# A two-layer transformer stack with routed experts on one core: expert weights fetched and given back in smaller parts

## The reference

```python
# H, F, E, K = 512, 800, 8, 2
logits = xt @ gate_w.T
probs = softmax(logits)
top_vals, top_idx = top_k(probs, K)            # 2 of 8 experts for each token
top_vals = top_vals / sum(top_vals)
h1 = einsum('th,efh->tef', xt, w1)             # up projections, 512 -> 800
h3 = einsum('th,efh->tef', xt, w3)
act = silu(h1) * h3
expert_out = einsum('tef,ehf->teh', act, w2)   # down projection, 800 -> 512
y = einsum('te,teh->th', w_full, expert_out)   # weighted sum over each token's two experts
# and in the stack: x = x + 0.5 * y
```

## Time and profile before

| | |
|---|---|
| runs | 1313.04, 1319.79, 1327.81 us; median 1319.79 us |
| profiled execution, its own time | 1325.27 us |
| its span, from the first to the last instruction | 1323.3 us |
| mean granted TensorE clock | 0.947 of full speed |
| TensorE busy | 1189.0 us (90%) |
| moe stages, first to last expert matmul | 212.30 to 514.6 us and 978.07 to 1299.7 us |
| moved by the SP queue (q1) | 148.50 MB |

### The profile page before, as it was taken

One profiled execution on the slowest core, in us unless ns is written; L12 is line 12 of the kernel. 1 busy time (PEld: TensorE's weight loads), 2 busy tenths in 40 slices (PEclk: granted clock), 3 DMA queues, 4 the chain that ended last, 5 costly groups with the idle time before them and its releaser, 6 DMA issues.

```text
span 1323.3 us, 26791 instructions
## 1 busy us (share of the span) xinstructions
PE 1189.0 (90%) x9913; PEld 509.8 (39%) x9913; DVE 871.6 (66%) x2479; ACT 357.2 (27%) x739; POOL 141.4 (11%) x191
## 2 busy tenths in 40 slices
PE   7799787999999995896899999998989899999982
PEld 4477463433333331342334433433634223333320
DVE  5731466877777762876788888851459576777753
ACT  5433520000000001331166666665200000000010
POOL 2200011111111100441000000000110010111000
PEclk9799779999999998998999999999989989999996
DMA  9000324158714254239604332004841644514555
GB/s 367 26 1 1 147 88 164 49 171 301 253 59 148 97 169 183 110 107 166 109 12 84 53 53 30 2 2 165 340 180 35 245 143 176 201 57 184 191 183 211
DMA packets 49017, 174.22 MB, mean 132 GB/s; under 512 B 8558, under 2 KB 15300, under 8 KB 44920
## 3 DMA queue, kind: packets, MB, share of 16 engines
q1 hardware_dynamic: 39679, 148.50, 34.9%
q0 software_dynamic: 5760, 18.88, 4.3%
q10 hardware_dynamic: 3448, 5.14, 1.1%
HBM read 785.47 MB, written 22.03 MB: 610 GB/s over the span
## 4 chain that ended last, share of the span: by engine, by line
PE 74%; DVE 10%; DMA 9%; issue 3%; ACT 3%; SPq 1%; ACTq 0%; POOL 0%; POOLq 0%; DVEq 0%
PE PS L1006 27%; PE PS L1024 13%; PE PS L1483 5%; PE PS L1446 5%; PE PS L1470 4%; DMA arena<-split_scratch 3%; PE PS L747 3%; DMA HH<-in_w 3%; PE PS L730 3%; PE PS L1510 2%; PE PS L1398 2%; PE PS L515 2%; DVE PS L1604 2%; PE PS L1035 1%; PE PS L529 1%
## 5 line engine op out<-in xcount | busy, mean ns | idle before, releaser
L1006 PE MATMUL PS<-arena 128*32 128x400 f32 x3456 | 395.8, 501 | 10.1 <-DMA HH<-in_w 6.1
L1006 PE MATMUL PS<-HH,arena 128*32 128x400 f32 x1152 | 395.2, 501 | 0.0
L1006 PEld LDWEIGHTS PS<-arena 128*32 128x32 f32 x3456 | 143.5, 110 | 256.4 <-issue 250.1
L1604 DVE CUSTOM_DVE_ANT_0 PS<-PS,U 128x128 f32<-128x128 f32 (+7 forms) x256 | 188.4, 782 | 43.9 <-PE PS L1446 42.3
L1190 DVE STREAM_TRANSPOSE arena<-arena 32x192 f32<-32x192 f32 x576 | 211.4, 367 | 7.2
L1024 PE MATMUL PS<-arena 128*32 128x512 f32 x1512 | 197.3, 604 | 11.6 <-DMA arena<-in_w2a 9.6
L1551 ACT ACTIVATE arena<-PS 128x512 f32<-128x512 f32 (+3 forms) x384 | 165.0, 497 | 74.5 <-PE PS L1473 48.9
L1168 DVE STREAM_TRANSPOSE arena<-arena 32x128 f32<-32x128 f32 x544 | 164.7, 303 | 17.1 <-DMA arena<-h_scratch,RT 9.2
L1062 ACT ACTIVATE arena<-PS 128x400 f32<-128x400 f32 x72 | 36.3, 504 | 442.3 <-PE PS L1006 442.3
L1174 DVE TENSOR_TENSOR arena<-arena,PS 128x400 f32<-128x400 f32 x72 | 40.9, 571 | 142.5 <-ACT arena L1062 142.4
L1006 PEld LDWEIGHTS PS<-HH,arena 128*32 128x32 f32 x1152 | 125.0, 110 | 0.0
(11 more groups left out here) (247 smaller groups left out, 1248.3 us busy)
## 6 DMA issues: line engine op xcount, KB each, us to landing
arena<-in_w SPq DMA_DIRECT2D x228, 1600.0 KB
arena<-in_w2a SPq DMA_DIRECT2D x114, 1536.0 KB
HH<-in_w SPq DMA_DIRECT2D x76, 1600.0 KB
HH<-in_w2a SPq DMA_DIRECT2D x38, 768.0 KB
arena<-in_w2a SPq DMA_DIRECT2D x38, 768.0 KB
arena<-split_scratch SPq DMA_DIRECT2D x60, 128.0 KB, 5.7
split_scratch<-arena SPq DMA_DIRECT2D x8, 768.0 KB, 5.9
arena<-in_w2b SPq DMA_DIRECT2D x72, 64.0 KB
```

Source lines behind the costliest of these rows:

```text
L1006: mm = eng.matmul(PS[SR * j:SR * j + SR, 2 * hf + m, 0:FH], XBT[:, u, c, SR * j:SR * j + SR], W13[j][:, c // 2, m, c % 2, hf * FH:(hf + 1) ...
L1604: eng.tensor_tensor_reduce(scores, scores, MASKW[:, T - wide:T], 1.0, HOLE, ALU.add, ALU.max, MP[:, g % 2, h, i:i + 1]).then_inc(S("s_md"), 1)
```

## The change

The up weights of a stream are now loaded in four parts, one for each c, each with its own semaphore, and TensorE raises m_wf after each of c = 0, 1, 2 (the last part is still given back with m_h at the end of up). The down weights are loaded in two halves, each with its own semaphore; TensorE raises the new m_w2f after the first three of its six parts, and waits for the second half only ahead of part 3. The bytes stay the same. An up load of one stream was 2 x 1600 KB with rows of 6400 B and is 4 x 800 KB with rows of 3200 B; the down weights of streams 0 to 2 were 1536 KB with rows of 12288 B and are 2 x 768 KB with rows of 6144 B (stream 3's were so before). `guess_in` uses the same smaller parts.

```diff
--- before.py
+++ after.py
@@ -821,13 +821,13 @@
 
 
         xg_in = [sem("xg_in0"), sem("xg_in1")]
-        w13_in = [sem("w13_in0"), sem("w13_in1")]
-        w2_in = sem("w2_in")
+        w13_in = [sem(f"w13_in{c}") for c in range(C)]
+        w2_in = [sem("w2_in0"), sem("w2_in1")]
         y_out = [sem("y_out0"), sem("y_out1")]
         yl_in = [sem(f"yl_in{i}") for i in range(NT)]
         LOADS = NSTEP + 1
         N13 = 16 * NSTR
-        N2 = 16 * (NSTR + 1)
+        N2 = 16 * NSTR
         N2B = 16 * NSTR
         w2b_in = [sem("w2b_in0"), sem("w2b_in1")]
         assert NSTEP % 2 == 0
@@ -846,21 +846,22 @@
             r = (j + p % 2) % NSTR
             return slice(SR * r, SR * r + SR)
 
-        def up_in(eng, j, a, e, cond=None):
-
-            eng.dma_start(W13[j][:, a].rearrange("p m c f -> p m (c f)"),
-                          A["w13"][e, :, :, 2 * a:2 * a + 2].rearrange("e p m c f -> p (e m) (c f)"),
-                          cond=cond).then_inc(w13_in[a], 16)
-
-        def down_in(eng, j, e, cond=None):
-
-            at = 0
-            for part in W2A[j]:
-                n = part.shape[1]
-                eng.dma_start(part.rearrange("p c d -> p (c d)"),
-                              A["w2a"][e, :, at:at + n].rearrange("e p c d -> p (e c d)"),
-                              cond=cond).then_inc(w2_in, 16)
-                at += n
+        def up_in(eng, j, c, e, cond=None):
+
+            eng.dma_start(W13[j][:, c // 2, :, c % 2], A["w13"][e, :, :, c].rearrange("e p m f -> p (e m) f"),
+                          cond=cond).then_inc(w13_in[c], 16)
+
+        def half_of(j, half):
+
+            if len(W2A[j]) == 2:
+                return W2A[j][half]
+            return W2A[j][0][:, half * FC // 2:(half + 1) * FC // 2]
+
+        def down_in(eng, j, half, e, cond=None):
+
+            eng.dma_start(half_of(j, half).rearrange("p c d -> p (c d)"),
+                          A["w2a"][e, :, half * FC // 2:(half + 1) * FC // 2].rearrange("e p c d -> p (e c d)"),
+                          cond=cond).then_inc(w2_in[half], 16)
 
         def tail_in(eng, p, j, e):
 
@@ -872,9 +873,10 @@
 
         def guess_in(eng, f, j):
 
-            for a in range(2):
-                up_in(eng, j, a, guess(j))
-            down_in(eng, j, guess(j))
+            for c in range(C):
+                up_in(eng, j, c, guess(j))
+            for half in range(2):
+                down_in(eng, j, half, guess(j))
 
         def sp_moe(eng, k, f):
             h, last = HS[k][0], 2 if f == 0 else 3
@@ -895,23 +897,26 @@
                         q = j * NSTEP + p
                         x = eng.value_load(EBX[q:q + 1, 0:1], min_val=0, max_val=2 * NE - 1)
                         now.append((bass.ds(x % NE, 1), x >= NE))
-                    for a in range(2):
+                    for c in range(C):
                         if p == 0:
-                            eng.wait_ge(w13_in[a], N13 * (LOADS * f + 1))
-                        elif a == 0:
-                            eng.wait_ge(S("m_wf"), NSTEP * f + p)
+                            eng.wait_ge(w13_in[c], N13 * (LOADS * f + 1))
                         else:
-                            eng.wait_ge(S("m_h"), 2 * (NSTEP * f + p))
+                            done = NSTEP * f + p - 1
+                            if c < C - 1:
+                                eng.wait_ge(S("m_wf"), (C - 1) * done + c + 1)
+                            else:
+                                eng.wait_ge(S("m_h"), 2 * done + 2)
                         for j in range(NSTR):
-                            up_in(eng, j, a, *now[j])
+                            up_in(eng, j, c, *now[j])
                 if p >= 1:
                     q = p - 1
-                    if q == 0:
-                        eng.wait_ge(w2_in, N2 * (LOADS * f + 1))
-                    else:
-                        eng.wait_ge(S("m_w2"), NSTEP * f + q)
-                    for j in range(NSTR):
-                        down_in(eng, j, *late[j])
+                    for half in range(2):
+                        if q == 0:
+                            eng.wait_ge(w2_in[half], N2 * (LOADS * f + 1))
+                        else:
+                            eng.wait_ge(S(("m_w2f", "m_w2")[half]), NSTEP * f + q)
+                        for j in range(NSTR):
+                            down_in(eng, j, half, *late[j])
                     if q >= 2:
                         eng.wait_ge(S("m_y"), NSTEP * f + y_done(q - 2))
                     for j in range(NSTR):
@@ -998,8 +1003,7 @@
                 if G > 0:
                     eng.wait_ge(S("m_act"), 2 * G)
                 for c in range(C):
-                    if c % 2 == 0:
-                        eng.wait_ge(w13_in[c // 2], N13 * (LOADS * f + p + 2))
+                    eng.wait_ge(w13_in[c], N13 * (LOADS * f + p + 2))
                     for hf in range(2):
                         for m in range(2):
                             for j in range(NSTR):
@@ -1009,20 +1013,24 @@
                                                 start=(c == 0), stop=(c == C - 1), skip_group_check=True)
                         if c == C - 1:
                             mm.then_inc(S("m_h"), 1)
-                    if c == 1:
+                    if c < C - 1:
                         mm.then_inc(S("m_wf"), 1)
 
             def down(p):
                 G, u = NSTEP * f + p, p % 2
-                eng.wait_ge(w2_in, N2 * (LOADS * f + p + 2))
                 eng.wait_ge(S("m_at"), G + 1)
                 if G >= 2:
                     eng.wait_ge(S("m_yc"), G - 1)
                 for c in range(FC):
+                    half = 2 * c // FC
+                    if c == half * FC // 2:
+                        eng.wait_ge(w2_in[half], N2 * (LOADS * f + p + 2))
                     for j in range(NSTR):
-                        part = W2A[j][c // W2A[j][0].shape[1]]
                         mm = eng.matmul(PS[SR * j:SR * j + SR, 4 + u, :], ACT_T[:, u, c, SR * j:SR * j + SR],
-                                        part[:, c % part.shape[1], :], start=(c == 0), stop=False, skip_group_check=True)
+                                        half_of(j, half)[:, c % (FC // 2), :], start=(c == 0), stop=False,
+                                        skip_group_check=True)
+                    if c == FC // 2 - 1:
+                        mm.then_inc(S("m_w2f"), 1)
                 mm.then_inc(S("m_w2"), 1)
                 if paired(p) and p % 2 == 0:
                     return
```

## The result

| | before | changed |
|---|---|---|
| median of the runs, us | 1324.3 (1313.04 to 1327.81, 6 runs) | 1306.75 (1304.39 to 1313.84, 6 runs) |
| ratio, with its 95% interval | | 0.9884 [0.9855, 0.9913] |
| profiled execution, own time, us | 1325.27 | 1311.64 |
| its mean granted TensorE clock | 0.947 | 0.952 |
| first moe stage, first to last expert matmul | 302.3 | 301.2 |

The kernel is 1.2% faster; 1305 was forecast. The profiled executions differ by 13.6 us, and the second moe stage alone by 13.5. The first gives 1.0, and about 1 is given back outside the two.

A forecast was written before the change was run, and what follows sets the result against it. TensorE was taken to bound the kernel, with gains only where it waits. Terms of 2.5 + 6.5 + 6.4 + 0.5 = 15.9 us took the median 1319.79 to 1303.9, stated as 1305; range 1298 to 1317.

The forecast's parts named there:

- A: In up(4) of the second moe stage, where two streams change expert, up weights by quarters win 2.5 us.
- B: In down(4) of the second stage, where two streams change, down halves end the wait and low clock: 6.5 us.
- C: In down(17), the second stage's last, where one stream changes, down halves remove idle time and low clock: 6.4 us.
- first stage: In the first moe stage the 0.5 us wait for up weights goes; the 2.0 us set by VectorE stay.
- a gap of 2.04 us left the clock full: At A, two gaps of some 2.4 us were taken to leave TensorE at full clock.
- The 1 us that I kept back for it: Allowance for the clock at A, taken off the summed gain to give 1305 us.
- margin of 1.9 us: At B, time by which the second down half was to land before TensorE needs it.
- More parts to issue: On SP, eleven more loads cost 4.3 us a step, hidden in 6.7 us of waiting, leaving 2.4; cost 0.
- 1, the low clock behind the gaps: Rival: clock stays low in the cut-up waits at A and C; won 11.3 us, 1308.5; chance 0.14.
- 2, SP as the bound: Rival: more issues make SP set the step; slower, 1365 or 1338 us; chance 0.05.
- 3, a fixed time for every DMA: Rival: parts pay some 2 us each in series at A, B and C; gain 2 us, 1318; chance 0.06.
- 4, less without the profiler: Rival: waits are shorter without the profiler, or cause the runs' spread; half the gain, 8 us, 1312; chance 0.13.

The follow-up runs named there:

- experiment 3: The changed kernel run once more with no edit; 1307.22 us, ratio 0.9898 to the kernel before.
- experiment 6: Changed kernel with SP reading each step's four expert numbers twice; the second of two runs measured 1355.17 us, ratio 1.0255.
- experiment 1: Kernel before with only the down weights by halves, up weights still in two halves; 1314.73 us, ratio 0.9899.
- experiment 4: Changed kernel with both down halves asked for only when all six parts of the down before are done; 1315.83 us, ratio 0.9941.
- first profile of 7: Changed kernel with SP reading the next step's expert numbers behind this step's up loads; two runs, 1306.74 us (ratio 0.9858) and 1304.89 us (0.988).
- 8 in the second: Changed kernel with expert numbers read ahead and w2b loads moved between c = 1 and c = 2 of the next up loads; 1304.33 us, ratio 0.9868.
- experiment 2: Kernel before with only the up weights by quarters, down weights as before; 1321.13 us, ratio 0.9985.
- Experiment 5: Changed kernel with TensorE waiting for both down halves ahead of down, still asked for by halves; 1311.13 us, ratio 0.9916.

## Why the prediction was right, and where it was not

Its terms in the profiled execution, us won:

| term | forecast | measured | how |
|---|---|---|---|
| A, up by quarters | 2.5 | 0.6 | A length 67.25 to 66.62 |
| B, down by halves | 6.5 | 6.5 | no wait, down at 5.15 |
| C, down by halves | 6.4 | 6.5 | C length 14.80 to 8.33 |
| first stage | 0.5 | 1.0 | 302.3 to 301.2 |
| elsewhere | 0 | -1.0 | the rest of 13.6; 0.8 of it between the two stages |
| sum | 15.9 | 13.6 | 1325.27 - 1311.64 |

The median, 1306.75 us, lies close to the 1305 partly by luck. The forecast started from 1319.79, the median of three runs, where all six have 1324.3; it had 14.8 us of gain, and the medians show 17.6.

**A** was mis-sized, and its bytes were not the reason. Counted from the stage's first matmul the last quarter was to land after 1052.3 - 978.07 = 74.2 us and landed after 1051.83 - 977.57 = 74.3; the gaps add up to 4.5 us, three of them (ahead of c = 1, 2 and 3), and I had two of some 2.4 ahead of c = 2 and 3. The term that failed is "a gap of 2.04 us left the clock full ... I take full". I read one row as a rule. The quarter behind the landing took 4.59 us instead of 2.7, and that is all of the 1.9 us missing. Where the clock held (experiment 3) the same code won 2.4. The length of the gap doesn't decide it by itself. Four kinds of gap, in both moe stages of ten profiles (experiment 6 left aside):

| gap, us | place | clock kept | clock fell |
|---|---|---|---|
| 0.67 or 0.68 | first matmul of a stage | 16 | 4 (experiments 1, 4 and the first profile of 7 in the first stage, 8 in the second) |
| 1.70 to 2.01 | A, quarters, ahead of c = 3, numbers not read ahead | 4 (experiments 2 to 5) | 1 (1.95, changed kernel) |
| 1.98 to 2.19 | last down, weights there in time | 12 | 4 (all 1.98: C in experiment 3, first stage in experiments 1, 4 and the first profile of 7) |
| 3.26 to 6.49 | waits for weights at A, B or C | 0 | 8 |

What decides it below 3 us stays open. So the term held in four of five profiles, with 2.0 to 2.9 us won at A, and failed in the one that is compared here. The 1 us that I kept back for it was about half the size of one such fall, 1.7 to 1.9 us.

**B** failed in no step. Experiment 5, which waits for both halves at the start, has no wait at B either, so the second half is early by more than the 2.6 us that TensorE needs for the first; the margin of 1.9 us that I worked out was too small. Asked for late (experiment 4), B waits only 1.28 us in its middle.

**C** was right by its mechanism: start set by VectorE, second half just in time. Both parts were taken away, one in each of experiments 4 and 5, and cost 4.1 and 4.8 us. Its margin of 0.2 us was as thin as forecast (0.82 us late in experiment 1, with the same down code).

**More parts to issue** cost nothing, as said, but for a smaller margin than worked out: 1.3 us a step left instead of 2.4, since the 11 additional issues took 6.7 - 1.3 = 5.4 us of SP's waiting and not 4.3: 0.49 us an issue, the three additional waits included, where I had 0.39. Both margins count the long waits; in an ordinary step 6.3 - 5.6 = 0.7 us is left.

**The first stage** won 1.0, all of it ahead of the second half of two ups: 0.7 at its up(4), where the forecast had only the 0.5 us of the waits list, and 0.3 at its up(16), a gap too short for that list. It isn't the quarters' alone: with the up loads as before (experiment 1) 0.1 of it is left, so the halves of the down weights take it away nearly as well. The second stage, forecast at 304 to 306 us, took 308.1, of which 1.9 are the fall at A.

**The rivals.** 1, the low clock behind the gaps: half true, it comes and goes at A and at C, one fall in each of the two profiles; both at once would have left a gain of 11.9 us, near its 11.3. 2, SP as the bound: its mechanism was shown in experiment 6, 2.7 us more in a step costs 47.9, but the change stops about 1 us a step short of it. 3, a fixed time for every DMA: false here. With rows of 3200 B and parts of 0.82 MB the share was 1.03 with 412 to 416 GB/s where parts of 1.64 MB moved 422; 1.4 to 2.4% slower is 0.2 to 0.4 us in 15.5, and I had taken 0.8. The Trainium skill, "DMA: Bandwidth & Descriptors", section on bandwidth, asks for at least 1 MiB in a DMA for 75% of peak, from DMAs issued by GpSimd. Here, where several DMAs of SP queue behind each other, the trace doesn't agree: parts below that size still moved 412 GB/s and more. 4, less without the profiler: false, the medians differ by 17.6 us (15.4 by the ratio) and the profiled executions by 13.6.

Experiments 1 and 2 add up: 1.01% and 0.15% against 1.16%, closer than intervals of 0.3% each can promise. The up quarters alone are within what can't be told from nothing; that they win 2 to 2.4 us at A is shown in profiles only. A profile's total is moved by the falls elsewhere too: the first stage of experiments 1, 4 and the first profile of 7 is 3.4 to 3.5 us longer than in the changed kernel, by two falls of 1.7.

## What to carry to other kernels

Where a consumer waits for a transfer into a single buffer, cut request and wait at the same points: at C the two together won 6.5 us, the late wait alone 2.4 and the early request alone 1.6. At B, with more time in hand, either of them did nearly all. If the queue is already full, as at A, smaller parts save only the work that is left behind the last byte, and an earlier first issue is worth as much again: reading the expert numbers ahead gave 2.3 us, the quarters 2 to 2.4. Count what the additional issues, empty ones too, take of the issuing engine's waiting in an ordinary step, without the long waits at the ends of a stage, and stop before it is used up.

## What was not expected of the hardware

- Idle gaps of TensorE of 0.68 and of 1.9 to 2.0 us are followed by the full clock in some executions and by half of it in others, at 1.98 us at the same instruction of the same program, while a gap of 2.19 us kept it and all of 3.26 us and more lost it. A fall behind one of the short gaps costs 1.7 to 1.9 us. The three profiles whose first stage began with a fall are also the only ones of the ten whose first stage ended with one; why is open.
- A skipped load isn't free for SP: 11 additional issues took 5.4 us in a step, 0.49 us each with three more waits, though nearly all moved nothing.
- Two executions, 3062.95 us in experiment 6 and 2305.74 in experiment 2, ran far slower than all others. In the first TensorE's up matmuls took 2.3 times as long (1168 ns in the mean for 501), while its granted clock is given as 1.00. Nothing here explains them.
